# The first attention's second chunk of scores and its exponentials placed directly behind the second token tile's projections

## The reference, cut to what matters

```python
x = layernorm(x + attn1(x))          # x: 8 sequences of 256 tokens, 128 channels
x = layernorm(x + ffn(x))

def attn1(x):                        # 16 query heads of 8 channels, one key and value head
    q, k = rope(x @ Wq + bq), rope(x @ Wk + bk);  v = x @ Wv + bv
    att = where(causal, -inf, q @ k.T / sqrt(8))       # (8, 16, 256, 256)
    return (softmax(att) @ v) @ Wo + bo

def ffn(x):
    h = x + attn2(rmsnorm(x, g1))    # 16 query heads of 64, 4 key and value heads, rope, causal
    return h + moe(rmsnorm(h, g2))   # 8 experts, 2 chosen per token, capacity 1/8 of the tokens
```

## Time and profile before

| | |
|---|---|
| time, median of 3 | 586.88 us |
| profiled execution | 582.76 us |
| its span, first to last instruction | 580.9 us |
| TensorE matmuls busy | 483.3 us (83%) |
| VectorE busy | 386.6 us (67%) |
| ScalarE busy | 229.6 us (40%) |
| GpSimd busy | 161.6 us (28%) |
| mean granted TensorE clock | 0.94 of 2.4 GHz |

### The profile page before, as it was taken

How to read it: one execution, slowest core, us unless ns; L and a number is a source line. 1 busy time by engine, 2 the same in 40 slices (tenths; PEclk the granted TensorE clock), 3 DMA queues, 4 the chain that set the end, 5 groups by cost and what they waited for, 6 DMA issues and landing times.

```text
span 580.9 us, 8112 instructions
## 1 busy us (share of the span) xinstructions
PE 483.3 (83%) x2788; PEld 266.4 (46%) x2788; DVE 386.6 (67%) x1096; ACT 229.6 (40%) x420; POOL 161.6 (28%) x200
## 2 busy tenths in 40 slices
PE   3776886899989989998999899999878689898920
PEld 2333453454354535544563555355354336565610
DVE  3518879657758675777668576766877544675785
ACT  1241442454383346425432742464133132445400
POOL 4210602400413230324202330403406542043531
PEclk9877997899999999999999999999979899999965
DMA  7400000000011003000300030030070332023223
GB/s 210 156 1 2 2 0 1 3 1 1 3 38 38 1 4 75 1 1 3 73 2 2 3 73 3 2 74 1 15 207 20 101 77 73 2 60 100 70 54 86
DMA packets 19093, 23.82 MB, mean 41 GB/s; under 512 B 2630, under 2 KB 15374, under 8 KB 18158
## 3 DMA queue, kind: packets, MB, share of 16 engines
q1 hardware_dynamic: 15308, 18.19, 11.8%
q0 software_dynamic: 1648, 4.07, 2.5%
q10 hardware_dynamic: 2098, 1.05, 0.6%
HBM read 16.71 MB, written 6.28 MB: 40 GB/s over the span
## 4 chain that ended last, share of the span: by engine, by line
PE 57%; DVE 19%; ACT 11%; issue 5%; DMA 4%; POOL 3%; ACTq 1%; POOLq 0%; DVEq 0%; SPq 0%
PE ps_r L929 7%; PE ps_st L894 6%; ACT pt L1689 5%; PE ps_r L803 4%; PE ps_r L661 4%; PE ps_st L883 4%; PE ps_r L956 4%; DVE rmax L1193 3%; PE ps_r L714 3%; DMA pt<-ys_dram,gidx 3%; PE ps_r L945 3%; PE ps_r L784 3%; DVE rmax_a L1193 2%; POOL qkr L554 2%; PE ps_st L1095 2%
## 5 line engine op out<-in xcount | busy, mean ns | idle before, releaser
L554 POOL TENSOR_TENSOR qkr<-qkr,prod 128x512 f32<-128x512 f32 (+1 forms) x48 | 52.3, 1093 | 211.6 <-DVE prod L1309 210.6
L1193 DVE TENSOR_REDUCE rmax_a<-ps_r 128x2 f32<-128x512 f32 (+1 forms) x96 | 61.5, 685 | 20.6 <-PE ps_r L784 20.3
L1193 DVE TENSOR_REDUCE rmax<-ps_r 128x2 f32<-128x512 f32 (+1 forms) x96 | 61.1, 684 | 11.5 <-PE ps_r L908 10.2
L661 PE MATMUL ps_r<-cbt 128*128 128x256 bf16 (+1 forms) x192 | 63.1, 328 | 4.9 <-DVE rmax_a L1193 2.4
L1689 ACT ACTIVATE pt<-ps_st 128x1024 f32<-128x1024 f32 x48 | 46.5, 1022 | 44.5 <-PE ps_st L699 44.1
L1698 ACT ACTIVATE pt<-ps_st 128x1024 f32<-128x1024 f32 x48 | 47.2, 1022 | 39.6 <-PE ps_st L894 39.6
L591 POOL TENSOR_TENSOR oT<-pvb,oT 128x1024 f32<-128x1024 f32 x14 | 33.3, 2400 | 94.7 <-DMA oT<-inv_dram 94.7
L929 PE MATMUL ps_r<-pt,vb 128*64 128x512 f32 x192 | 48.5, 611 | 4.9 <-ACT pt L1698 3.2
L956 PE MATMUL ps_r<-wqkv,xT_b 128*128 128x512 f32 x96 | 45.9, 616 | 3.8 <-DVE rmax_a L1193 3.2
L784 PE MATMUL ps_r<-kq_a 128*128 128x512 f32 x96 | 45.7, 535 | 0.0
L661 PEld LDWEIGHTS ps_r<-cbt 128*128 128x128 bf16 x192 | 18.9, 99 | 48.7 <-issue 31.9
(11 more groups left out here) (237 smaller groups left out, 901.1 us busy)
## 6 DMA issues: line engine op xcount, KB each, us to landing
oT<-inv_dram SPq DMA_DIRECT2D x14, 512.0 KB, 5.8
xs_dram<-pvb SPq DMA_DIRECT2D x1, 2048.0 KB
pt<-in_L_ffn_w SPq DMA_DIRECT2D x2, 1024.0 KB, 7.0
ys_dram<-qkr SPq DMA_DIRECT2D x14, 128.0 KB
qkr<-xs_dram POOLq DMA_DIRECT2D x4, 256.0 KB, 3.8
x_all<-in_L_attn_x ACTq DMA_DIRECT2D x1, 896.0 KB, 8.2
pvb<-xs_dram POOLq DMA_DIRECT2D x3, 256.0 KB, 4.3
out<-x_all SPq DMA_DIRECT2D x1, 640.0 KB, 3.8
```

The source lines that it names most:

```text
L554: nc.gpsimd.tensor_tensor(part, part, prod[:, (3 * t + i) % 2, 0:w], ALU.add).then_inc(add_in, 1)
L661: nc.tensor.matmul(o[:, :, P * (i >= 4):], ident_b, qmask.unsqueeze(1).broadcast_to([P, heads, P]), start=True, stop=False, skip_group_che ...
L1193: nc.vector.tensor_reduce(heads_of(i), ps_r[:, b, :].rearrange("p (h k) -> p h k", h=4 if i < 4 else 2), AX.X, ALU.max).then_inc(free[b], 1)
```

## The change

On TensorE `scores_a(s, 1)` moves from behind `turn_tokens` to directly behind `project(s, 1)`; on ScalarE the two exponentials of this chunk, `exp_a(s, 2)` and `exp_a(s, 3)`, move from behind `turned_tokens` to directly behind `take_weights(s, 1)`. Nothing is added or removed, and the waits of each instruction are the same ones.

```diff
@@ TensorE, step(s)
                 maxima(s, 8, 12)
                 if "PB" in on:
                     project(s, 1)
+                if "SA" in on:
+                    scores_a(s, 1)
                 if "MB" in on:
                     max_rows(s)
                 if "PA" in on:
...
                     project_a(s)
                 if "TB" in on and s < NB - 1:
                     turn_tokens(s)
-                if "SA" in on:
-                    scores_a(s, 1)
                 if "PB" in on:
                     turn_qk(s, 0)
@@ ScalarE, step(s)
                 neg_max_a(s, 1)
                 take_weights(s, 1)
+                if "SA" in on:
+                    exp_a(s, 2)
+                    exp_a(s, 3)
                 if "MB" in on:
                     neg_max(s)
...
                     take_values_a(s, 0)
                 if "TB" in on and s < NB - 1:
                     turned_tokens(s)
-                if "SA" in on:
-                    exp_a(s, 2)
-                    exp_a(s, 3)
                 if "PB" in on:
                     high_parts(s, 0)
```

## The result

| | before | changed |
|---|---|---|
| time, median | 587.17 us (585.63 to 590.11, 4 runs) | 579.17 us (574.61 to 580.65, 4 runs) |
| ratio, with its 95% interval | | 0.984 (0.980 to 0.988) |
| profiled execution, span | 582.76, 580.9 us | 579.19, 577.3 us |
| mean granted TensorE clock | 0.940 | 0.947 |

The change makes the kernel faster, by 8 us where 3.4 were forecast. Executions more than 1.5% above the fastest of the same kernel are left out of every ratio here, though not out of the medians, so that a ratio need not be the quotient of two medians (seven of e4's twelve are such, its profiled one among them).

The account below looks back on a forecast made before the run. TensorE bounds the kernel, with some 2.4 us per step to be had around the change. Terms -4.1 - 0.6 - 0.3 + 0.3 + 1.3 = -3.4 us from 586.88 give 583.5 us; range 580.7 to 586.4, 8 in 10.

Parts of the forecast that it names:

- steady step: Steps 0 to 3: third chunk's exponentials and L714 start 1.03 us earlier in each, 4.1 us gained in all.
- step -1: Same queue order but VectorE less behind, 2.50 us from L916 to L750; masks earlier, 0.6 us gained.
- step -3: TensorE waits for the DMA, then masks wait for `qkv`; 1.3 us lost, with the clock left open.
- step -2: VectorE does not hold `qkv` for long, L750 waits for `xT_a` behind the exponentials; 0.3 us lost.
- step 4: No `qkv`, so L965 still waits for VectorE's release of `p12`; masks slightly earlier, 0.3 us gained.
- the clock stays up: Step -3: TensorE's clock stays at the upper level, gaining 0.7 us instead of losing 1.3; within a rival of chance 0.14.
- The stages behind step 4 only shift: Expert part and gathers behind step 4 keep their lengths and only start earlier; no term in the sum.
- The DMA is late: Rival: the transfer of tile 1's maxima takes 3.28 us and TensorE waits; +5.5 us, 592.4 us, chance 0.10.
- The gain is given back: Rival: low-clock stretches in steps -3 to -1, or half the steady gain, bring about 585.8 us; chance 0.20.
- Early steps cheap: Rival: clock in step -3 stays up, -0.7 in place of +1.3, later stretches alike; 581.5 us, chance 0.14.

Follow-up runs that it names:

- e4: Changed kernel with TensorE in the new order but ScalarE in the order of before; 587.41 us, ratio 0.996 to the kernel before.
- pair of one chip: Further profiled executions of the unedited kernel before and changed kernel on one chip (f3, f1), also called second pair; spans 578.4 and 571.3 us.
- first pair: The original profiled executions of the kernel before and the changed kernel; spans 580.9 and 577.3 us.
- e3: The change in steps -3 and -2 alone, later steps in the order of before; 589.57 us, ratio 1.005 to the kernel before.
- f3: The kernel before again, without an edit, for a second profile; 580.65 us, ratio 1.001.
- e6: The kernel before with 20 further unused mask matmuls on TensorE in each of steps -2 and -1; 576.75 us, ratio 0.993.
- f1: The changed kernel again, without an edit, on the third chip; 573.83 us, ratio 0.990 to the kernel before.
- e5: Changed kernel with ScalarE's two small copies (negated maxima, transposed input) between the second chunk's two exponentials; 571.37 us, ratio 0.984 to the kernel before.
- f2: Changed kernel with the two small copies between the exponentials, as in e5, on another chip; 570.43 us, ratio 0.986 to the kernel before.
- e8: Changed kernel with the DMA of tile 1's maxima ahead of the two of the sums in SyncE's queue; 570.64 us, ratio 0.984 to the kernel before.
- e1: The changed kernel again, without an edit, for its profile and more timed runs; 579.63 us, ratio 0.986 to the kernel before.
- f4: Changed kernel with two further unused DMAs ahead of the one of tile 1's maxima from step 0 on; 575.19 us, ratio 0.993 to the kernel before.

## Why the prediction missed

The mechanism was right and its direction too; the sum was too small, -3.4 where the pair of one chip has -7.5 in steps -3 to 4. Taken from 586.88 that is 579.4, which is below the range as well. So the miss does not hang on the scatter of the timed runs. What failed are sizes of the sum: of the 4.1 us that it lacks, the four steady steps hold 1.3, step -1 1.3, step -3 0.8, step -2 0.5 and step 4 0.2. By the steps of the prediction:

**The steady step, -1.03: measured -1.20 to -1.34, and -1.46 in step 0.** This was the largest term, and all four together miss by 1.2 us in the first pair and 1.3 in the second. The order of events is as forecast, in every joint; the lengths are shorter. From the chunk to L750 3.04 where 3.21 was forecast, from L750 to L965 0.96 for 1.08, from L965 to the masks 1.25 for 1.31, and the rest as forecast: 0.36 in sum (0.1 of it lost again, since the chunk starts later behind the projections than L916 did). For 0.23 of it the reason is how I used the rows. I added the lengths of successive instructions (1.95 + 0.27 + 0.38 + 0.05), but instructions of one engine overlap in the rows: the exponentials start at 260.89 for 1.94, that is to 262.83, and `negmax` starts at 262.71; `negmax` lasts to 262.96, and `xT_a` starts at 262.87. Distances between starts would have given less. The same holds for TensorE: L965 has 1.31 in the earlier trace rows, and the masks start 1.25 behind it where nothing is waited for. The 0.12 between L750 and L965 are not of this kind, since I had worked with distances there: with the chunk gone, L965 starts closer behind L812 than the chunk did (264.34 - 264.12 = 0.22 us, against 268.26 - 267.95 = 0.31), and the rest is open.

**Step -1, -0.6: measured -1.9 in the pair of one chip, -2.5 in the first.** This term failed most. I took VectorE to be less behind there, 2.50 us from L916 to L750. In e3 and f3, which have the old order in this step, it is as much as in a steady step. e3:

```profile
106.57 0.27 PE L916 MATMUL ps_r<-cft,rmax 128*32 128x128 f32 x1
...
109.52 0.51 PE L750 MATMUL ps_r<-wa,xT_a 128*128 128x144 f32 x2 [0.27 <-DVE prod L1311]
```

That is 2.95, and in f3 it is 2.94. The execution that I read had TensorE at the lower level just ahead of that place, and f3 had not. Before, then f3 (TensorE alone: stretch, length, busy, clock, DMA share, GB/s):

```profile
102.09:105.50 3.41, 3.41 (x9) 0.50 0.03 10
```

```profile
102.09:105.50 3.41, 2.98 (x13) 1.00 0.02 7
```

In that stretch stand the projections: L916 starts 3.34 us behind the first of them in the execution that I read (103.96 to 107.30) and 2.57 in f3 (104.05 to 106.62). A slower TensorE delays its own L916 while VectorE goes on, and so VectorE's lag looks small. e6, the fourth execution with this order in step -1, bears it out: it too had TensorE at the lower level just ahead of the place (0.51 from 99.20 to 102.60), and the distance is 2.50 again (104.86 to 107.36), with L916 2.95 us behind the first projection. With 2.94, step -1 is a steady step, and my own working gives -1.0 for it. From the place behind the projections to the second values it is 10.00 us in f3:

```profile
106.62 0.27 PE L916 MATMUL ps_r<-cft,rmax 128*32 128x128 f32 x1
...
116.62 1.92 PE L714 MATMUL ps_r<-pt,va 128*32 128x512 f32 x16 [0.95 <-ACT pt L1689]
```

and 8.45 in f1, 1.55 less:

```profile
106.61 0.50 PE L699 MATMUL ps_st<-kq_a 25*128 25x512 f32 x4
...
115.06 1.92 PE L714 MATMUL ps_r<-pt,va 128*32 128x512 f32 x16 [0.88 <-ACT pt L1689]
```

The same distance shrank by as much in step 0. The last 0.3 of the 1.88 lie ahead of the changed place: from the step's first transposes to L791 it is 25.08 us in f3 (77.44 to 102.52) and 24.67 in f1, but 24.54 in the first profile of before, so two executions of one program differ there by more than this. Against e3, whose step -1 is 41.56, the gain is 1.5.

**Step 4, -0.3: measured -0.50 (-0.47 in the first pair).** As forecast L965 waits for VectorE and stays; its tail is shorter than its row, as above. After:

```profile
368.88 1.31 PE L965 MATMUL ps_r<-cft,qkr 128*128 128x128 f32 x10 [0.78 <-DVE prod L1309]
370.03 1.03 PE L696 MATMUL ps_st<-cbt 128*128 128x512 bf16 x4
```

1.15 from one start to the next.

**Step -2, +0.3: measured -0.1 to -0.2.** The step's weak point was seen rightly, L750 waits for `xT_a` with nothing to cover it:

```profile
69.97 0.48 PE L750 MATMUL ps_r<-wa,xT_a 128*128 128x144 f32 x2 [1.02 <-ACT xT_a L1713]
71.80 1.03 PE L696 MATMUL ps_st<-cbt 128*128 128x512 bf16 x4
```

But from there to the masks it takes 1.83 where I put 2.17, and the loss is gone. e5 and f2 show the weak point's price: with the copies between the exponentials this step is 0.93 shorter. 

**Step -3, +1.3: measured +1.25 in the first pair, +0.52 in the second.** The wait for the DMA came as forecast, 2.18 us, and the chunk within 0.1 us of the place worked out. That the first pair meets the forecast is partly luck: the masks come 1.84 us later than before (35.28 against 33.44), and 0.81 of this is made good before L714, where the masks and scores ran at the lower level before and at the upper one after (masks 1.56 and 1.04). In the second pair the step of before is 0.3 longer and that of the changed kernel 0.4 shorter, with the lower clock at other places. After:

```profile
30.96 0.50 PE L699 MATMUL ps_st<-kq_a 25*128 25x512 f32 x4 [2.18 <-DMA kq_a<-nega]
...
35.28 1.04 PE L696 MATMUL ps_st<-cbt 128*128 128x512 bf16 x4
38.88 3.51 PE L714 MATMUL ps_r<-pt,va 128*32 128x512 f32 x16 [2.12 <-ACT pt L1689]
```

The masks come 0.6 later than the place worked out, since L750 too runs at the lower level (0.82 us in place of 0.48). L714 stays there as well, as forecast, in six of the seven executions that have this order in step -3. In e8, the seventh, it did not:

```profile
37.21 1.92 PE L713 MATMUL ps_r<-pt,va 128*32 128x512 f32 x16 [2.12 <-ACT pt L1688]
```

and the step took 25.40, shorter than any of before. Not all of this is L714's: 1.5 us of the difference to the first profile of the changed kernel lie ahead of L791, where the order is the old one (from the step's first transposes 12.44 us in e8, 13.92 there). From L791 to the step's end it is 12.96 us, against 14.73 in the changed kernel and 13.52 in the kernel before. So what I kept as a rival (the clock stays up) does happen, in one execution and not in another, the new pattern of pauses does not settle it, and its gain of 0.56 us on the kernel before is near the 0.7 that I gave it. The Trainium skill's rule (TensorE: Matmul & The Clock Gate, What's actually happening), that the low clock is the default and activity lifts it, agrees with the six; it did not tell which of two executions of one order gets through.

**What lies around the sum.** "The stages behind step 4 only shift" holds for the pair of one chip (-0.09 and -0.27). In the first pair the gain ahead of the experts was 9.25 us, and 5.7 of it were gone by the last expert matmul. The rows there name no instruction as the cause. After, the chain of waits:

```profile
511.54 2.77 another core or an unknown queue
```

The longer expert part is not the change's, since e1 and f1 (58.01, 56.68) do not have it. What makes the experts take 55 to 63 us in one and the same code stays open.

**The rivals.** The DMA is late: in the steady steps it is not, e8 shows that an earlier one brings nothing, and f4 that 0.24 us were to spare (the forecast had 0.2) and that what is beyond it is lost (0.68 us late, 0.64 to 0.72 longer). I put 0.10 on it; given 0.2 us of margin that was not too much. With the trace's 1.81 the transfer issued at 258.23 lands 0.30 ahead of the chunk. With the fixed cost of about 2.0 us that the Trainium skill gives for GpSimd's path (DMA: Bandwidth & Descriptors, Anatomy of one DMA — SWDGE (gpsimd) path) it would land at 260.23, an estimate, 0.11 ahead; f4's 0.24 lies between the two. The gain is given back: the opposite came, the terms were larger than forecast. Early steps cheap: steps -3 to -1 together were indeed cheaper than forecast (-1.57 in the second pair, -1.34 in the first, for +1.0), but mostly for another reason than the rival's, the misread lag in step -1 and the shorter tails; only in step -3 of the second pair may it be the clock.

**The range** was built from spread in the clock and from the unknown DMA. It had nothing for a bias that all steps share. Four steady steps and step -1 have one mechanism, so an error of 0.3 in it counts five times; a range that took this in would have reached 1.5 us lower, to 579.2, where the measured time lies.

## What to carry to other kernels

Work out a moved chain from distances between starts of instructions, not from the lengths in the rows, above all where the sum is taken several times over: here 0.23 us per step of a term of 1.03 was tail that overlaps. Read a step's waits from a stretch at the upper clock, or from the same step in a second execution, before taking them as a property of the order. Where long instructions pass short copies in an in-order queue (ScalarE's here), ask of every step what covers the copies: in the step without cover, placing them between the two exponentials brought 0.93 us, in the steady ones 0.1.

## What the runs showed of the hardware

The lower level of TensorE's clock falls at other places in executions of one program. Beside the stretch at 102 us above, the kernel before had it at 419.53 in its first profile and not in f3, in the same program:

```profile
419.53:426.35 6.82, 6.43 (x28) 0.50 0.94 297
```

```profile
419.53:426.35 6.82, 6.29 (x46) 1.00 0.94 296
```

From step 5's L916 to step 6's it took 42.79 us in the one and 39.59 in the other, and the changed kernel 41.16 and 39.58. So over 3 us can appear in one pair of profiles that no edit made, and five runs of the changed kernel on one chip (e1) spread from 574.47 to 580.32 us.

With 40 matmuls of work that nobody needs, the kernel before ran 0.7% faster (e6). From 44 to 120 us, steps -2 and -1, it was granted 0.98 of the clock, against 0.89 and 0.91 in the two profiles without them, and did more work there in less time: what the lower clock cost in these steps was more than the matmuls. The 1.6 to 2.2 us that the two steps gave are part of the 4.1 us; the rest was not placed.

The wait from the issue of the DMA to the chunk that needs it was 261.84 - 259.97 = 1.87 us in f4, where TensorE waited for it, close to the 1.81 of the earlier trace rows.
